# A four-layer graph network on one core: the bias of the last layer written into the result banks by ScalarE, two pieces of work moved between engines, and a new order of the edge stage

## The reference, cut to what matters

```
hi = x @ W1[:128];  hj = x @ W1[128:]
h  = relu(hi[i] + hj[j] + b1)          # for every pair (i, j)
y  = layernorm(h @ W2 + b2) * gamma + beta
out[i] = sum over j of adj[i, j] * y[i, j]
```

## Time and profile before

| | |
|---|---|
| time, median of 3 runs | 458.41 us (458.27 to 459.51) |
| span of the profiled execution | 459.2 us |
| busy share: PE, PEld, DVE, ACT, POOL | 96%, 90%, 91%, 84%, 77% |
| granted TensorE clock, mean | 0.987 |

### The profile page before, as it was taken

How to read it: one execution, slowest core, us unless ns; L and a number is a source line. 1 busy time by engine, 2 the same in 40 slices (tenths; PEclk the granted TensorE clock), 3 DMA queues, 4 the chain that set the end, 5 groups by cost and what they waited for, 6 DMA issues and landing times. The chain is left out here.

```text
span 459.2 us, 14175 instructions
## 1 busy us (share of the span) xinstructions
PE 440.2 (96%) x3420; PEld 414.6 (90%) x3453; DVE 416.2 (91%) x1523; ACT 386.5 (84%) x1003; POOL 354.0 (77%) x651
## 2 busy tenths in 40 slices
PE   8699989999999999999999999999999999999993
PEld 3599989999999999889998999999999999999991
DVE  6989999999999999996898898899889888989975
ACT  2368979999999899998788888888888888888874
POOL 4569979999999899756677787777768676868762
PEclk9889999999999999999999999999999999999997
DMA  7134344445444652233313222232223131313111
GB/s 221 41 83 131 95 139 161 153 151 178 154 148 156 221 190 77 76 109 121 122 55 99 69 74 80 69 85 63 91 60 94 51 103 51 103 51 86 37 46 49
DMA packets 50939, 47.60 MB, mean 104 GB/s; under 512 B 5584, under 2 KB 42576, under 8 KB 50896
## 3 DMA queue, kind: packets, MB, share of 16 engines
q1 hardware_dynamic: 49760, 46.45, 33.2%
q10 hardware_dynamic: 1136, 0.66, 0.5%
HBM read 28.22 MB, written 18.87 MB: 103 GB/s over the span
## 5 line engine op out<-in xcount | busy, mean ns | idle before, releaser
L1593 PEld LDWEIGHTS bank<-w2c,hE 128*128 128x128 f32 x512 | 67.3, 192 | 2.4
L1593 PE MATMUL bank<-w2c,hE 128*128 128x128 f32 x512 | 67.5, 275 | 0.2
L905 ACT ACTIVATE hE<-bank,front 128x512 f32<-128x512 f32 x64 | 44.2, 691 | 7.6 <-PE bank L1574 7.4
L927 ACT ACTIVATE sqE<-bank 128x512 f32<-128x512 f32 x63 | 37.7, 599 | 12.8 <-PE bank L1593 12.3
L1237 DVE TENSOR_REDUCE ssum<-sqE 128x4 f32<-128x512 f32 x63 | 42.6, 676 | 4.3 <-ACT sqE L927 2.9
L706 POOL TENSOR_TENSOR gHl<-gH,gHu 128x512 fp32r<-128x512 f32 x32 | 41.0, 1283 | 5.6 <-ACT gHu L879 5.6
L1104 DVE BATCH_NORM_STATS2 stats<-t 128x6 f32<-128x128 f32 x192 | 44.4, 272 | 1.0 <-issue 1.0
L1262 DVE TENSOR_TENSOR ym<-bank,wE 128x512 f32<-128x512 f32 x64 | 43.2, 681 | 1.6 <-POOL wE L755 0.3
L722 POOL TENSOR_TENSOR half<-ym 128x512 f32<-128x512 f32 x31 | 39.5, 1273 | 3.3 <-DVE ym L1262 3.1
L1591 PE MATMUL bank<-bias,ones_b 128*128 128x512 bf16 x92 | 35.0, 380 | 0.7 <-DVE ym L1262 0.6
L1593 PEld LDWEIGHTS bank<-w2c,hC 128*128 128x128 f32 x256 | 33.6, 192 | 1.3
(11 more groups left out here) (191 smaller groups left out, 1624.6 us busy)
## 6 DMA issues: line engine op xcount, KB each, us to landing
hh_scratch<-hh SPq DMA_DIRECT2D x32, 256.0 KB, 2.2
gH<-hh_scratch SPq DMA_DIRECT2D x32, 256.0 KB, 2.8
A<-adj_groups SPq DMA_DIRECT2D x32, 128.0 KB, 2.1
res_scratch<-res SPq DMA_DIRECT2D x32, 128.0 KB, 2.1
gRES<-res_scratch SPq DMA_DIRECT2D x32, 128.0 KB, 2.5
AT<-adjT_groups SPq DMA_DIRECT2D x31, 128.0 KB, 2.3
out<-y SPq DMA_DIRECT2D x30, 128.0 KB, 1.9
X<-x_groups SPq DMA_DIRECT2D x29, 128.0 KB, 2.2
```

The lines of the kernel that those rows point to most:

```text
L905: nc.scalar.activation(hE[g][:, :], HE_ps, ACT.Relu, bias=C["L3_b1"]).then_inc(b[f"hE{g}_ready"], 1)
L927: nc.scalar.activation(sqE[g][:, :, :], YE_ps[g], ACT.Square).then_inc(b[f"sqE{g}_ready"], 1)
L1593: last = nc.tensor.matmul(ps[:, i, :], hidden[:, i * P:(i + 1) * P], w2c[:, :], start=False, stop=i == tiles - 1)
```

## The change

- `project` no longer issues the bias product for units 1 to 31. Instead three new ACT stages, `sd0`, `sd1` and `sdc`, copy the bias row `b2c`, spread to 128x512, from SBUF into the result banks (`seed_ell`, `seed_csr`). Each waits until DVE has read the bank for the last time (`ymE0_ready`, `ymE1_ready`, `yC_ready` of the unit before), and the products of `m0`, `m1`, `mc` wait for the seed. Unit 0 keeps the bias product.
- `keep_Q` leaves ACT. DVE does it in one instruction, `row_places`: `Q_ps` plus `off2`, 128x256.
- `split_upper` leaves ACT. POOL does it with a `tensor_copy` right behind `hs`.
- `T3` and `FIRST` are new. `FIRST` covers units 0 to 7.

```diff
-        T3 = {"idx": 0, "T": 2.44, "spu": 3.82, "hs": 6.51, "beg": 7.08, "Qp": 7.27, "rows": 8.02, "spl": 8.21, "kS": 11.23, "V": 11.89,
...
+        T3 = {"idx": 13.81, "rows": 24.1, "V": 27.72, "cols": 30.52, "g0": 29, "g1": 31.32, "gc": 31.26, "m0": 31.6, "m1": 32.98, "mc": 32.27,
+              "sc": 43.91, "kS": 21.13, "kST": 25.17, "r0": 25, "r1": 27.72, "rc": 26.03, "sd0": 25.33, "sd1": 28.45, "sdc": 27.69, "s0": 28.56,
+              "s1": 29.94, "sqc": 29.23, "std": 32.13, "fstd": 47.34, "app": 56.01, "beg": 19.97, "T": 13.73, "Qp": 14.43, "T2": 25.5, "d0": 31.33,
+              "d1": 32.46, "dc": 31.89, "rec": 34.43, "x0": 35.34, "x1": 36.51, "yn": 35.92, "tot": 42.82, "st": 45.1, "ag": 47.4, "frec": 55.15,
+              "spl": 24.59, "hs": 16.69, "a1": 39.12, "a2": 39.45, "gm": 42.97, "rs": 44.28, "w": 34.2, "om": 55.2, "sh": 56.15}
...
-            edge_stages = [(("idx", 0.5), next_ot), (("spl", "hs", 1.5), next_h), (("rs", 0.8), next_res), (("app", 1), store)]
+            edge_stages = [(("idx", 0.5), next_ot), (("spl", 1.5), next_h), (("rs", 0.8), next_res), (("app", 1), store)]
...
                 wait_past(pool, b["HE1_psum"], count(2))
+                wait_past(pool, b["HC_psum"], count(2))
                 nc.gpsimd.tensor_tensor(hs[q][:, :, :], gH[q][:, :, 0:P], gH[q][:, :, P:2 * P], ALU.add).then_inc(b["hs_ready"], 1)
+                nc.gpsimd.tensor_copy(gHu[q][:, :, :], gH[q][:, :, :]).then_inc(b["split_up"], 1)
...
-            def split_upper(q, u, count):
...
-            def keep_Q(q, u, count):
...
+            def seed_ell(g):
+                def stage(q, u, count):
+                    if isinstance(u, int) and u == 0:
+                        return
+                    act.wait_ge(b[f"ymE{g}_ready"], count(1))
+                    nc.scalar.activation(YE_ps[g], b2c[:, :].unsqueeze(1).to_broadcast([P, ELL, P]), ACT.Copy).then_inc(b[f"seedE{g}_done"], 1)
+                return stage
+
+            def seed_csr(q, u, count):
+                if isinstance(u, int) and u == 0:
+                    return
+                act.wait_ge(b["yC_ready"], count(1))
+                nc.scalar.activation(YC_ps, b2c[:, :].unsqueeze(1).to_broadcast([P, GROUP * CSR, P]), ACT.Copy).then_inc(b["seedC_done"], 1)
...
+            def row_places(q, u, count):
+
+                if isinstance(u, int) and u == 0:
+                    dve.wait_ge(off_ready, 1)
+                dve.wait_ge(b["TE_ready"], count())
+                wait_past(dve, b["V_psum"], count(2))
+                nc.vector.tensor_tensor(Qp[q][:, :, :], Q_ps, off2[:, bass.ds(u * GROUP, GROUP)].unsqueeze(2).to_broadcast([P, GROUP, P]),
+                                        ALU.add).then_inc(b["Qp_ready"], 1)
...
-            def project(ps, hidden, tiles, done):
-                nc.tensor.matmul(run(ps), ones_b[:, :], run(bias3[:, :, :]), start=True, stop=False)
+            def project(ps, hidden, tiles, done, seeded=False):
+                if not seeded:
+                    nc.tensor.matmul(run(ps), ones_b[:, :], run(bias3[:, :, :]), start=True, stop=False)
                 for i in range(tiles):
-                    last = nc.tensor.matmul(ps[:, i, :], hidden[:, i * P:(i + 1) * P], w2c[:, :], start=False, stop=i == tiles - 1)
+                    last = nc.tensor.matmul(ps[:, i, :], hidden[:, i * P:(i + 1) * P], w2c[:, :], start=False, stop=i == tiles - 1, skip_group_check=seeded)
                 last.then_inc(b[done], 1)
...
-                    wait_past(pe, b[f"ymE{g}_ready"], count(1))
-                    project(YE_ps[g], hE[g], ELL, f"YE{g}_psum")
+                    seeded = not (isinstance(u, int) and u == 0)
+                    if seeded:
+                        pe.wait_ge(b[f"seedE{g}_done"], count(1))
+                    else:
+                        wait_past(pe, b[f"ymE{g}_ready"], count(1))
+                    project(YE_ps[g], hE[g], ELL, f"YE{g}_psum", seeded)
```

More of the change, by code:

```diff
@@ L305, in gnn_stack @@
                   "esd_ready", "erstd_ready", "wE_ready", "ymE0_ready", "ymE1_ready", "yC_ready", "O_psum", "half_done", "accE_ready",
-                  "tot_ready", "gout_done", "tout_ready", "ostats_done", "omv_ready", "omean_ready", "ostd_ready", "orstd_done", "oshift_ready", "out_ready"]
+                  "tot_ready", "gout_done", "tout_ready", "ostats_done", "omv_ready", "omean_ready", "ostd_ready", "orstd_done", "oshift_ready", "out_ready", "seedE0_done", "seedE1_done", "seedC_done"]
         b = {n: sem("u_" + n) for n in names3}
@@ L364, in wait_past @@
                 engine.wait_ge(semaphore, n)
-        T3 = {"idx": 0, "T": 2.44, "spu": 3.82, "hs": 6.51, "beg": 7.08, "Qp": 7.27, "rows": 8.02, "spl": 8.21, "kS": 11.23, "V": 11.89,
[4 rows of a table removed]
-              "app": 49.01}
+        T3 = {"idx": 13.81, "rows": 24.1, "V": 27.72, "cols": 30.52, "g0": 29, "g1": 31.32, "gc": 31.26, "m0": 31.6, "m1": 32.98, "mc": 32.27,
[4 rows of a table added]
         AGES = 4
         START3, EARLY, CATCH = 216.0, 5.0, 25.0
[L376 to L380, removed]
[7 rows of a table removed]
-                 ("beg", 2): 225.69, ("beg", 3): 240.58, ("beg", 4): 244.47, ("beg", 5): 247.21, ("rows", 0): 219.62, ("rows", 1): 225.56,
-                 ("rows", 2): 229.73, ("rows", 3): 243.06, ("rows", 4): 251.45, ("rows", 5): 263.45, ("s1", 0): 220.31, ("s1", 1): 234.83,
[4 rows of a table removed]
-                 ("cols", 0): 223.8, ("cols", 1): 228.19, ("cols", 2): 236.96, ("cols", 3): 246.55, ("cols", 4): 261.85, ("cols", 5): 272.97,
-                 ("gc", 0): 224.76, ("gc", 1): 229.1, ("gc", 2): 238.28, ("gc", 3): 247.38, ("gc", 4): 261.99, ("gc", 5): 274.28, ("kST", 0): 225.01,
-                 ("kST", 1): 228.65, ("kST", 2): 242.85, ("kST", 3): 249.8, ("kST", 4): 262.68, ("kST", 5): 273.1, ("rc", 0): 226.69,
[5 rows of a table removed]
-                 ("std", 3): 262.55, ("std", 4): 275.09, ("std", 5): 281.29, ("rec", 0): 229.34, ("rec", 1): 239.04, ("rec", 2): 246.8,
[9 rows of a table removed]
-                 ("fstd", 3): 281.1, ("frec", 0): 268.55, ("frec", 1): 276.47, ("frec", 2): 280.71, ("frec", 3): 281.94, ("om", 0): 271.08,
-                 ("om", 1): 276.44, ("om", 2): 277.25, ("sh", 0): 271.19, ("sh", 1): 277.18, ("sh", 2): 280.73, ("app", 0): 272.51,
-                 ("app", 1): 277.83, ("app", 2): 281.76}
@@ new lines, in gnn_stack @@
+        FIRST = {("Qp", 0): 219.28, ("Qp", 1): 222.44, ("Qp", 2): 228.92, ("Qp", 3): 234.32, ("Qp", 4): 246.17, ("Qp", 5): 262.43, ("Qp", 6): 283.83,
[7 rows of a table added]
+                 ("app", 0): 261.45, ("app", 1): 292.81, ("app", 2): 314.99, ("app", 3): 320.4, ("app", 4): 345.53, ("app", 5): 355.03,
+                 ("app", 6): 361.33, ("app", 7): 374.96, ("beg", 0): 219.72, ("beg", 1): 224.91, ("beg", 2): 225.77, ("beg", 3): 244.77,
+                 ("beg", 4): 254.33, ("beg", 5): 263.35, ("beg", 6): 327.22, ("beg", 7): 403.81, ("cols", 0): 223.83, ("cols", 1): 228.72,
+                 ("cols", 2): 234.75, ("cols", 3): 250.27, ("cols", 4): 265.17, ("cols", 5): 266.93, ("cols", 6): 295.4, ("cols", 7): 306.76,
[4 rows of a table added]
+                 ("frec", 3): 337.58, ("frec", 4): 339.59, ("frec", 5): 345.28, ("frec", 6): 362.33, ("frec", 7): 371.58, ("fstd", 0): 248.43,
+                 ("fstd", 1): 280.73, ("fstd", 2): 286.28, ("fstd", 3): 339.47, ("fstd", 4): 345.13, ("fstd", 5): 373.62, ("fstd", 6): 373.9,
[6 rows of a table added]
+                 ("idx", 0): 198.08, ("idx", 1): 219.07, ("idx", 2): 226.82, ("idx", 3): 230.38, ("idx", 4): 242.15, ("idx", 5): 254.27,
+                 ("idx", 6): 269.42, ("idx", 7): 306.12, ("kS", 0): 221, ("kS", 1): 226.42, ("kS", 2): 231.82, ("kS", 3): 244.61, ("kS", 4): 253.92,
+                 ("kS", 5): 271.1, ("kS", 6): 311.52, ("kS", 7): 327.11, ("kST", 0): 224.03, ("kST", 1): 228.81, ("kST", 2): 243.48,
+                 ("kST", 3): 251.87, ("kST", 4): 262.98, ("kST", 5): 287.03, ("kST", 6): 321.9, ("kST", 7): 330.5, ("m0", 0): 218.3,
[8 rows of a table added]
+                 ("rec", 1): 237.57, ("rec", 2): 254.14, ("rec", 3): 268.03, ("rec", 4): 318.16, ("rec", 5): 320.5, ("rec", 6): 375.43,
+                 ("rec", 7): 389, ("rows", 0): 220.29, ("rows", 1): 225.9, ("rows", 2): 230.34, ("rows", 3): 248.34, ("rows", 4): 253.73,
[8 rows of a table added]
+                 ("sdc", 1): 233.21, ("sdc", 2): 240.57, ("sdc", 3): 254.46, ("sdc", 4): 272.35, ("sdc", 5): 304.7, ("sdc", 6): 318.87,
+                 ("sdc", 7): 386.45, ("sh", 0): 276.39, ("sh", 1): 300.96, ("sh", 2): 335.83, ("sh", 3): 343.19, ("sh", 4): 344.02,
+                 ("sh", 5): 389.41, ("sh", 6): 402.57, ("sh", 7): 402.88, ("spl", 0): 212.16, ("spl", 1): 220.96, ("spl", 2): 228.79,
+                 ("spl", 3): 239.34, ("spl", 4): 247.85, ("spl", 5): 257.18, ("spl", 6): 279.57, ("spl", 7): 311.87, ("sqc", 0): 228.74,
```

(30 more changed lines are left out.)

## The result

The changed kernel takes 473.28 us (median of 4; 471.39 to 473.84) against 458.74 (median of 4) for the kernel of before, measured beside it: a ratio of 1.0302, 95% interval 1.0273 to 1.0330. The forecast was 457.6 in a range of 450.5 to 466. The profiled execution took 473.84; its span is 472.1 where it was 459.2. The mean granted clock is 0.988 where it was 0.987, so the clock has no part in it.

The account below looks back on a forecast made before the run. The prediction took the ring through ACT, 7.53 a unit, plus DVE's turn and friction as the bound, 15.74 a pass. Loop +1.1, before it -0.7, behind it -1.2 sum to -0.8: 457.6 us, range 450.5 to 466.

Parts of the forecast that it names:

- DVE needs 7.13 + 0.34 = 7.47: DVE's work per unit: 7.13 as before plus 0.34 for the added 128x256 operation out of a bank.
- the ring through ACT: Closed chain from `s1` of one unit to the next, through DVE, `x0`, the seeds and ACT's steps: 7.53 a unit.
- The forecast's signs: If right: passes of 15.6 to 15.9, ACT over 93% busy, PE waiting for ACT, DVE idle before `T` eleven times.
- The third rival: DVE's round bounds: 7.67 a unit plus the turn, `begun` slow in both units, 16.2 a pass, 462.7 us; chance 0.13.
- The turn: DVE's loop turn between `d1` and `T2`, on the ring once in two units: 0.58 a pass left exposed.
- the first rival: DVE's sequencer runs ahead of `d1` and the turn hides: 15.16 a pass, 451 us; chance 0.26.
- The seed's pitch: Each ACT copy of 512 bias columns into a bank, three a unit: 0.52, a quarter of the way from 0.49 to 0.62.
- `Qp` on DVE: The 128x256 operation out of a bank that DVE gains: 0.34 a unit, taken from `tot`, ends 0.34 and 0.42.
- POOL's copy: The 512-column copy that POOL gains: 0.74, costing nothing unless it exceeds about 1.3.
- PE's 0.63: Three bias products a unit at 0.21 each leave PE, which would then need 7.19 of its 7.82 a unit.

Follow-up runs that it names:

- the eighth run: Changed kernel with `begun` in its new place but comparing 258 numbers as three gapped rows of 86: 455.80 us, ratio 0.9939 to the kernel of before.
- run 1: Changed kernel with `begun` moved from 19.97 to 17.5 in the edge order, between `T` and the reciprocal: 469.93 us, ratio 1.0248.
- run 8: The same as the eighth run: changed kernel with `begun` in its new place, comparing three gapped rows of 86: 455.80 us, ratio 0.9939.
- Run 9: Changed kernel with `begun` at 17.5 as in run 1, and all edge-order places 3.5 earlier against the loop's body: 462.66 us, ratio 1.0093.
- run 7: Changed kernel with the copy of the upper halves back on ACT, POOL without it: 477.22 us, ratio 1.0394.
- runs 10 and 12: 10: changed kernel with the three-row comparison and edge places 3.5 earlier, 450.41 us; 12: that kernel with the bias products back on PE, 457.90 us.
- 5 and 6: 5: changed kernel with `begun` between `x0` and `x1`, 471.90 us; 6: the same with `kS` later and `std` earlier on ACT, 475.37 us.
- run 4: Changed kernel with the row places' offsets added on ACT again, two activations a unit: 467.63 us, ratio 1.0170.

## Why the prediction was wrong

**The step that failed: "DVE needs 7.13 + 0.34 = 7.47."** The 7.13 carried `begun` at its old price, a mean pitch of 0.66 for the pair (0.52 and 0.80 in the earlier trace rows), to a new place. Behind `x1`, beside `half`, its pitch is 1.56. Summed start to start, the unit has 8.13 of work, 1.56 of it `begun`; at 0.66 it would be 7.23, and with the mean wait of 0.25 for the weights 7.48. The collision adds 0.90 a unit, 1.80 a pass: 2 x 7.48 + 1.80 = 16.76, measured 16.74. (This adds up the same rows; the test is the eighth run, which takes the wait away.) With it the path went too: not the ring through ACT, 7.53, but DVE's own round sets the pass. The forecast's signs say so: passes of 16.74 and not 15.6 to 15.9, ACT busy 89% and not over 93%, no idle time before `T`, and PE waiting 27 times for DVE's `T` and only twice for a seed. The forecast priced the added work at its new place and carried the moved pair at its old length.

**The third rival had the mechanism and mis-sized it.** "DVE's own round is the bound", with "the pair `begun` ... slow in both", charged 0.28 a pass, as if 0.88 were the worst; it was 1.80. The earlier trace rows had the price: a second comparison shut out by `half` waits up to 1.27. The prediction says that nothing shows which POOL instruction stood beside the longer `begun` of before. The timeline of POOL does:

```profile
300.49 1.27 POOL L706 TENSOR_TENSOR gHl<-gH,gHu 128x512 fp32r<-128x512 f32 x1
```

The pair of 0.88 (301.29 in the earlier trace rows) starts 0.47 before the end of `gHl`, so it met only the tail of such an instruction, and 0.88 was no worst case. The rows of before could not have told that `half` starts right behind `begun`, but the order could: `half` waits for the weighing that `begun` follows.

**The turn.** The forecast put 0.58 a pass on the ring. In the changed kernel nothing of it shows, as the first rival had it, and that lowers the time: in this term the forecast erred the other way. In run 1 `d1` waits for ACT right ahead of the turn, and the longer unit is 0.75 longer. In run 8 it is 0.61 longer, although DVE stands start to start from the weighing `x0` to `d1` as in the changed kernel; why the turn shows there is open. Run 9 shows that moving the loop's cut takes it away.

**What held.** The seed's pitch, 0.52 taken and 0.52 to 0.54 measured, above `ST`'s 0.49, so no cheaper write into a bank shows; `Qp` on DVE, 0.34 taken and measured; POOL's copy, 0.74 taken, 0.61 measured, and off the path (run 7). The ring, 7.53: run 1 shows 7.91 with the pair's 0.53 in it, so 7.38. The 0.15 lies in ACT's stretch from `sd0` to `s1`, 4.15 (341.63 to 345.78) for 4.30, most of it in S, pitch 0.48 for 0.61. Without the collision (run 8) the change makes a pass of 15.65 and 455.8 us, where the forecast had 15.74 and 457.6. That this is so close is in part luck: there too DVE waits only for POOL's weights, 0.16 or 0.34, so that the 7.52 of the shorter unit is its own round and not the ring, and the pair in it is dearer than the forecast's. PE's 0.63 was hidden behind DVE; of it 0.25 a unit is shown as time (runs 10 and 12).

## What to carry to other kernels

When an order changes, price every moved instruction again by what stands beside it on the other engine: here two VectorE comparisons from SBUF to SBUF went from 0.53 to 1.56 beside one GpSimd addition of 1.27. If such an operation can't be moved (runs 1, 5 and 6 each found another wait), a shape that does not wait is worth trying, even if it is dearer alone. And choose where a loop is cut: the same order with the cut elsewhere took 15.83 a pass in place of 16.58 (run 9 against run 1).

## What the runs showed of the hardware that was not expected

- The same comparison costs 0.26 a piece in the plain shape of 256 (0.53 from the pair's start to the next operation) and 0.39 in the shape of 3 x 86 (0.78), but beside a POOL operation of 1.27 the plain pair takes 1.56 and the other still 0.78.
- The collision goes both ways: with the comparisons first, POOL's `half` took 1.39 and its 128x2 operation 0.30, against 1.27 and 0.20.
- A loop turn of DVE showed as 1.07 of idle time (before), 0.48 (run 1), 0.37 (run 8), 0.23 (run 4) or nothing (the changed kernel, run 9). What decides between these is not parted by the runs.
